# The keys' sums of a linear-attention kernel: rounded parts, two tiles behind the projections

## The reference, cut to what matters

```
k  = einsum('bnd,dhk->bnhk', x, Wk)                 # "key", 1024 columns a token
dd = einsum('bnhd,md->bnhm', k * dn, proj)          # "dash", 1024 columns a token
kf = exp(dd - sum(k*k)*dn*dn/2 - max(dd)) + eps     # features, 1024 a token
kv = einsum('bnhm,bnhd->bhmd', kf, v)               # v = x @ Wv
ks = sum(kf, axis=1)
```

## Time and profile before

| | us |
|---|---|
| median of 3 runs | 1642.57 (1641.53 to 1649.5) |
| profiled execution, its own time | 1645.18 |
| profiled execution, span of the trace | 1643.5 |
| TensorE busy | 1479.6 (90%) |
| VectorE busy | 1167.2 (71%) |
| ScalarE busy | 698.2 (42%) |
| GpSimd busy | 536.0 (33%) |
| keys' block, first DMA to last VectorE instruction | 513.37 to 869.32 |

### The profile page before, as it was taken

How to read it: one execution, slowest core, us unless ns; L and a number is a source line. 1 busy time by engine, 2 the same in 40 slices (tenths; PEclk the granted TensorE clock), 3 DMA queues, 4 the chain that set the end, 5 groups by cost and what they waited for, 6 DMA issues and landing times. The chain is left out here.

```text
span 1643.5 us, 23406 instructions
## 1 busy us (share of the span) xinstructions
PE 1479.6 (90%) x8607; PEld 1219.5 (74%) x8607; DVE 1167.2 (71%) x2252; ACT 698.2 (42%) x1291; POOL 536.0 (33%) x520
## 2 busy tenths in 40 slices
PE   8876659999991899999986999999998999989997
PEld 6443549999991666666645788888887889979996
DVE  6665885774003678878638878787886888899995
ACT  2054125546552132222222333333345777767774
POOL 2412025555551022222314000000004555547666
PEclk8877669999995799999998999999999999999999
DMA  6544819999954011111013000000103100000001
GB/s 205 232 162 163 282 59 277 269 294 277 286 137 138 26 39 39 39 39 39 26 52 115 1 26 27 26 26 27 65 13 93 52 27 14 1 1 27 14 27 39
DMA packets 121777, 152.00 MB, mean 92 GB/s; under 512 B 13584, under 2 KB 89528, under 8 KB 120640
## 3 DMA queue, kind: packets, MB, share of 16 engines
q1 hardware_dynamic: 108448, 129.55, 24.0%
q0 software_dynamic: 9216, 12.59, 4.3%
q10 hardware_dynamic: 4000, 8.37, 1.4%
HBM read 116.10 MB, written 33.60 MB: 91 GB/s over the span
## 5 line engine op out<-in xcount | busy, mean ns | idle before, releaser
L2357 POOL TENSOR_TENSOR ff_hid_lo<-ff_hid,ff_hid_hi 128x512 fp32r<-128x512 f32 x128 | 174.3, 1365 | 159.1 <-ACT ff_hid_hi L2269 157.7
L1230 PE MATMUL h_ps<-xT,w 128*128 128x128 f32 x1536 | 203.9, 287 | 1.1 <-ACT xT L938 1.1
L1230 PEld LDWEIGHTS h_ps<-xT,w 128*128 128x128 f32 x1536 | 191.0, 199 | 9.5 <-issue 9.5
L2638 PE MATMUL ff_down<-ff_w_hi,ff_hid_hi 128*128 128x256 f32 x512 | 146.8, 287 | 7.6 <-POOL ff_hid_lo L2357 4.5
L2639 PE MATMUL ff_down<-ff_w_lo,ff_hid_hi 128*128 128x256 f32 x512 | 145.3, 284 | 0.0
L2640 PE MATMUL ff_down<-ff_w_hi,ff_hid_lo 128*128 128x256 f32 x512 | 145.2, 284 | 0.0
L1344 PE MATMUL k_ring<-w_hi,hT_hi 128*128 128x512 f32 x256 | 120.0, 469 | 10.7 <-DVE hT_lo L1504 6.4
L1685 PE MATMUL k_acc<-wide_rows,hk 128*128 128x512 f32 x256 | 119.7, 599 | 4.5 <-ACT wide_rows L1629 4.5
L1111 DVE TENSOR_TENSOR yT<-yT_ps,b2T 128x256 f32<-128x256 f32 x48 | 20.4, 425 | 140.4 <-PE yT_ps L1244 137.3
L1344 PE MATMUL q_ring<-w_hi,hT_hi 128*128 128x512 f32 x256 | 109.9, 429 | 9.9 <-PEq L99 6.8
L2044 PE MATMUL q_out_ps<-kv_sums,wide_rows 128*128 128x256 f32 x512 | 115.5, 379 | 0.0
(11 more groups left out here) (436 smaller groups left out, 3620.4 us busy)
## 6 DMA issues: line engine op xcount, KB each, us to landing
w<-in_L_ffn_W_dram SPq DMA_DIRECT2D x48, 1024.0 KB, 6.0
w<-in_L_ffn_W_dram SPq DMA_DIRECT2D x48, 256.0 KB, 7.8
expert_sum_dram<-f_zero SPq DMA_DIRECT2D x8, 1024.0 KB, 15.3
x<-in_L_attn_x_dram SPq DMA_DIRECT2D x4, 1024.0 KB, 13.2
h_dram<-hg SPq DMA_DIRECT2D x8, 512.0 KB, 2.9
hk<-expert_sum_dram SPq DMA_DIRECT2D x8, 512.0 KB, 4.5
hT_hi<-expert_sum_dram SPq DMA_DIRECT2D x8, 512.0 KB, 5.4
h_dram<-hk SPq DMA_DIRECT2D x8, 512.0 KB, 6.1
```

The source lines that it names most:

```text
L1230: last = pe.matmul(h_ps[:, e % 2, s * KD + c, :], w1[:, e % RING, s, k, c::KD], xT[:, e % 2, k, :], start=(k == 0), stop=(k == KD - 1))
L2357: pool.tensor_tensor(hid_lo[:, m % PARTS, :], hid[:, m % WHOLES, :], hid_hi[:, m % PARTS, :].bitcast(F32), ALU.subtract).then_inc(part_low, 1)
L2638: pe.matmul(into, hid_hi[:, m % PARTS, tile], high[:, c, :], start=(c == 0 and j % 2 == 0), stop=False)
```

## The change

In the keys' block:

- `sums` takes f32 operands no more. ACT rounds the features into `features_hi` (`feature_high`) and the rows into `hk_hi` (`rows_high`); GpSimd subtracts to get `features_lo` (`feature_low`), DVE to get `hk_lo` (`rows_low`), both in place of the features and rows. A sum is then `split_products`, three products of parts for one f32 product.
- The sums of a tile stand two tiles later: `late = n * G + j - 2`. A counter `tile_summed` per tile replaces `sums_done` per group. `features_hi` has room for two tiles.
- The maximum over partitions is made by TensorE (`peak_turn`, `spread_peak`) in place of GpSimd. `turn(n+2)` stands before the last dash of the window, `total(n-1)` in window n.
- Group 0 is made ready tile by tile (`tile_sums` and so on), group 1's rows are joined on GpSimd (`group_sums`).

Outside it: the keys' weights are loaded and cut during the last experts (`key_high`, `key_low`), the experts' block ends without a drain of GpSimd, constants of the networks are made during the experts (`wave_angles`, `elu_rows`), the ring of expert weights is shifted by three slots, and in the queries' block GpSimd's products and sums wait for `normed` and come in smaller pieces.

The core of the diff:

```
-                    if n >= KV_RING:
-                        sp.wait_ge(sums_done, n - KV_RING + 1)
+                        sp.wait_ge(tile_summed, (n - KV_RING + 1) * G)
                         sp.wait_ge(h_out[n % KV_RING], 16 * (n // KV_RING))
                     sp.dma_start(hk[:, n % KV_RING], rows(g.expert_sums[0])).then_inc(first_in[n % KV_RING], 16)
...
                 for n in range(NG):
-                    peak_of(n)
                     if n + 2 < NG:
                         power(n + 2)
-                    add_features(n)
+                    add_first(n)
+                    if n < NG - 1:
+                        feature_low(n, 0)
+                        feature_low(n, 1)
+                    for j in range(2, G):
+                        add_feature(n, j)
+                        if n < NG - 1:
+                            feature_low(n, j)
...
+                def feature_low(n, j):
+                    pool.wait_ge(e_high_done, n * G + j + 1)
+                    pool.tensor_tensor(e_low[:, n % 2, j, :], dash[:, n % 2, j, :], e_high(n * G + j).bitcast(F32),
+                                       ALU.subtract).then_inc(e_low_done, 1)
...
+                def feature_high(n, j):
+                    i = n * G + j
+                    act.wait_ge(exp_done, i + 1)
+                    if i >= 2:
+                        act.wait_ge(tile_summed, i - 1)
+                    act.activation(e_high(i), dash[:, n % 2, j, :], ACT.Copy).then_inc(e_high_done, 1)
...
-                def sums(n, j, k):
+                def sums(i, k):
+                    n, j = i // G, i % G
                     if k == 0:
-                        pe.wait_ge(exp_done, n * G + j + 1)
+                        pe.wait_ge(e_low_done, i + 1)
...
-                        last = pe.matmul(acc[:, k, cols], hk[:, n % KV_RING, j, k * P:(k + 1) * P], dash[:, n % 2, j, cols],
-                                         start=(j == 0), stop=(j == G - 1))
+                        last = split_products(pe, acc[:, k, cols], rows, features, cols, j == 0, j == G - 1)
+                    if k == KD - 1:
+                        last.then_inc(tile_summed, 1)
...
                 for n in range(-1, NG):
                     for j in range(G):
-                        i = (n + 1) * G + j
+                        i, late = (n + 1) * G + j, n * G + j - 2
                         if n + 1 < NG:
                             project("key", i, key_done)
-                        if n >= 0 and j:
-                            sums(n, j - 1, 0)
+                        if n >= 0 and j == 0:
+                            peak_turn(n)
+                        if j == G - 1 and n + 2 < NG:
+                            turn(n + 2)
+                        if late >= 0:
+                            sums(late, 0)
+                        if n >= 0 and j == 0:
+                            spread_peak(n)
+                            if n:
+                                total(n - 1)
                         if n + 1 < NG:
                             project("dash", i, dash_done)
-                        if n >= 0 and j:
-                            sums(n, j - 1, 1)
+                        if late >= 0:
+                            sums(late, 1)
```

More of the change, by code:

```diff
@@ L596, with wave_tables @@
 FOLD_SLOT, ELU_SLOT, WAVE_SLOT = 3, 5, 7
+CONSTS_AT = 32
+B1, THETA, W_RE, W_IM, AMP, SINE, COSINE = range(7)
+TURN = 1.0 / (2.0 * 3.141592653589793)
+FULL = 6.283184
+STEP = 0.1 * TURN
+def wave_tables(g):
+    part = g.flip[:, 0:2 * CF].rearrange("p (i c) -> p i c", i=2)
+    return [part] + [g.flip[:, 2 * CF + i * CF * B:2 * CF + (i + 1) * CF * B].rearrange("p (c b) -> p c b", b=B) for i in range(3)]
 def expert_choice(nc, mk, g, a):
@@ L1359, in key_ring_order @@
 def key_ring_order():
-    order = [("turn", 0)]
+    order = []
     for n in range(-1, NG):
@@ new lines, in _ @@
+                tile_sums(0)
+                tile_statistics(0)
+                tile_sums(1)
+                tile_rows(0)
+                tile_statistics(1)
+                tile_sums(2)
+                tile_turned_low(0)
+                tile_rows(1)
+                tile_statistics(2)
+                tile_sums(3)
+                tile_rows(2)
+                tile_turned_low(1)
+                tile_statistics(3)
+                diag(0)
+                shift(0)
+                tile_rows(3)
@@ L1587, in _ @@
+                tile_turned_low(2)
+                for n in range(-1, NG - 1):
                     for j in range(G):
                         i = (n + 1) * G + j
-                        diag(i)
-                        shift(i)
-                        if n >= 0 and n + 2 < NG:
-                            if j == 0:
+                        if i:
+                            diag(i)
+                        if j == 0 and n >= 0:
+                            refer(n)
+                            if n:
+                                add_total(n - 1)
+                        if j == G - 1 and n + 2 < NG:
+                            turned_low(n + 2)
+                        if i:
+                            shift(i)
+                        if i == 1:
+                            tile_turned_low(3)
+                            v.mark(dve.tensor_reduce(f.h_sum[:, 0, :], first_sum[:].rearrange("p j k -> p k j"), AX.X, ALU.add))
+                        if j == 0 and n >= 0:
+                            rows_low(n)
+                        if j == 1 and n >= 1:
+                            add_sums(n - 1)
+                        if n + 2 < NG:
+                            if n < 0 and j == 1:
+                                dve.wait_ge(summed, 3)
+                                statistics(1)
+                            elif n < 0 and j == 2:
+                                rows(1)
+                            elif n < 0:
+                                pass
+                            elif j == 0:
@@ L1602, in _ @@
+                refer(NG - 1)
+                add_total(NG - 2)
+                rows_low(NG - 1)
+                add_sums(NG - 2)
+                for j in range(G):
+                    last_feature_low(j)
+                for i in range(2, 4):
+                    weights_low(i, next_raw)
+                turned_low(NG)
                 add_sums(NG - 1)
+                add_total(NG - 1)
             @block.scalar
@@ L1642, in _ @@
                             turned_high(n + 2)
-                turned_high(NG)
+                        if n >= 0:
+                            feature_high(n, j)
+                        if j == G - 1 and n + 1 < NG:
+                            rows_high(n + 1)
                 act.wait_ge(next_in, 32)
@@ L1654, in take, with tile_turn @@
                         kind, i = order[u - 2]
-                        pe.wait_ge(freed[kind], i + 1)
+                        pe.wait_ge(freed[kind], i if kind == "turn" else i + 1)
+                def tile_turn(j):
+                    pe.wait_ge(tile_h, j + 1)
+                    for k in range(KD):
+                        last = pe.transpose(first_turn[:, j, k], hk[:, 0, j, k * P:(k + 1) * P], g.ident[:])
+                    last.then_inc(tile_turned, 1)
                 def turn(n):
```

423 lines of the change are left out of this document (267 added, 156 removed).

## The result

The changed kernel takes 1782.45 us (median of 4 runs, 1780.64 to 1784.17), the kernel before 1642.13 (4 runs, 1641.53 to 1649.5). The ratio is 1.0834, with a 95% interval of 1.0812 to 1.0857: slower by 140 us, where 161 were forecast. The profiled execution of the changed kernel has a span of 1782.4 us.

What follows compares the result with a forecast made beforehand. TensorE was taken as the bound, 38.4 us a window; new waits make windows 1 to 5 +158 us, and all terms +161 on 1645.2 give 1806, less 2.6 for the median: 1803 us, range 1735 to 1838.

Steps and rivals of the forecast that it cites:

- start, to the end of window -1: Keys' block opening: missing drain gives 4 us, then 48 us from the loads; 558 against 565.9, so -8 us.
- window 0: First full window: no wait for the load but one for power's, slow restarts; 54 us against 37.4, +16.6.
- windows 1 to 5: Keys' block: five windows of 70 us each against 38.4, +158 us.
- queries and networks: Later stages: GpSimd's pieces no longer meet VectorE's, constants made earlier, less ScalarE's cuts of weights; -3 us.
- cycle: Windows 1 to 5, one D1 to the next: waits in a row, 70.5 us counted, 70 taken, bounds 59.5 and 75.5.
- D1: End of the dash of tile 1 in a window, from which the forecast times each step; D2, D3 likewise for tiles 2, 3.
- restart at the lower clock: TensorE after each idle time: 6.1 us at half speed, 3 us of work lost.
- rows beside GpSimd: VectorE's rows(n+2), 3.9 us with GpSimd idle, plus two waits of 2.5 for GpSimd's instructions; bounds none and four.
- saving of the products: TensorE's sums: 16 f32 products a window replaced by products of parts, 2.8 us off, 36.1 us a window if nothing waits.
- waits as forecast, but clock and port cost nothing: Rival, 12%: no lower clock or port waits; windows of 59.5 us, window 0 of 43, total 1740.
- the load isn't waited for: Rival, 10%: only power ahead of the low parts holds TensorE; cycle 59.4 us, total about 1750.
- Faster: Rival, 8%: low parts and loads in time, low part 0 within 4.1 us of D1; windows 36.1 us, total 1616.

Runs made afterwards that it cites:

- e0: The kernel before, unaltered, run and profiled a second time: 1642.53 us, span 1640.8.
- e1: Changed kernel with VectorE's both_sums(n+2) moved behind the shift of tile 1 and add_sums, directly ahead of join(n+2): 1751.83 us.
- e4: Changed kernel with the experts' first part landing in the free half of hT_lo, both loads issued at the window's start: 1732.15 us.
- e13: Changed kernel with 36 useless TensorE products ahead of tile 0's first half sum in each window from 0 on, except window 6: 1769.72 us.
- e6: Changed kernel with loads issued at the window's start, VectorE's calls reordered and GpSimd's power between the low parts of tiles 0 and 1: 1639.35 us.
- e10: e6 with rows_low a window earlier behind tile 2's shift, rows_high one tile sooner, tile 0's first half sum behind tile 2's dash: 1634.44 us.
- e11: e10 with GpSimd's power(n+2) back at the head of its list for the window: 1653.99 us.
- e9: Changed kernel with the queries' GpSimd additions again four of 128 x 2048 that start at once, without waits for normed: 1789.21 us.

## Why the prediction was right, and where it was off

By its own steps, with the profiled executions (in us; the change from the first profile of the kernel before, and from the second, e0's):

| step | forecast | against the first | against e0's |
|---|---|---|---|
| start, to the end of window -1 | -8 | -2.8 | -8.8 |
| window 0 | +16.6 | +12.0 | +14.9 |
| windows 1 to 5 | +158 | +149.3 | +149.3 |
| window 6 | -3 | -2.6 | -2.6 |
| the block's end | 0 | -1.0 | -2.0 |
| queries and networks | -3 | -16.0 | -9.2 |
| sum | +161 | +138.9 | +141.6 |

**The cycle was right step by step.** From D1, forecast and measured in the window shown: landing taken up 7.5 and 7.0; statistics done 19.3 and 19.0; low part 0 done 25.5 and 24.7; D2 32.5 and 31.0; rows done 43.9 and 41.5; D3 51.9 and 48.8; next D1 70.5 and 68.1. TensorE's two idle times are 20.6 (some 21) and 6.3 (7.3). That both waits in the chain are real, and that they come one behind the other, e1 to e4 show: taking either away gives 6.8 to 10.3 us a window, both together 17.2 and, with the rows in time, 27. The queue of VectorE cost what its rows said, and `feature_low`, 2.6 taken between 2.4 and 6.7, is 2.33.

**Two terms of the cycle were too large.** The restart at the lower clock was priced at 3 us, half of the 6.1 us at clock 0.50 in the earlier trace rows. Those rows are right, with 14 products at half speed behind waits of 4.29 and 2.77 us, but they don't carry over. Here it costs 2.1: ten products 0.43 apart where 0.23 would do, and a period 2.1 us shorter in e13. In e6 and e10 it costs 1.6. What sets the number was not tried; it doesn't grow with the wait in front. The first restart of the window shown:

```profile
724.80:729.40 4.60, 4.58 (x11) 3.63 (x12) 0.00 (x0) 0.00 (x0) 4.60 (x2) 0.52 0.00 0
729.40:735.40 6.00, 5.96 (x26) 4.53 (x25) 4.12 (x4) 1.06 (x2) 1.56 (x2) 1.00 0.00 0
```

And the rows beside GpSimd were priced at two waits of 2.5: the four TENSOR_SCALAR took 5.52 for 1.38, so 4.1 were lost. The four began at 733.55 and the last ended at 739.07, 0.5 us behind the second of the two GpSimd instructions that stand there back to back (733.88 and 736.21): VectorE was held by both. The Trainium skill (SBUF — State Buffer, Who interferes with whom) adds that reductions never contend; the trace agrees, with 1.23 us for the one of e11 at 709.09, beside GpSimd's addition of 708.45 to 710.85. The prediction's bound of 15 us for the rows, had each of the six instructions met one of GpSimd, wasn't reached: 8.0.

**The saving of the products was too large by a quarter.** Window 6 of the changed kernel, full and at full clock, is 35.76 us without a turn, where the one before, with a turn of 0.87 in it, was 38.4. So a window's work on TensorE is 36.6 us, not 36.1: 1.75 less than before, where 2.3 were counted. This changes little in the forecast's cycle, whose length the waits set, but it lowers what the change could ever give: some 12 us, not 16, in seven windows.

**The start was right by its own steps.** From the last scatter's issue to the keys' first load it was 10.6 us (502.79 to 513.37, and 10.5 in e0) and is now 6.1, so the missing drain gave what was counted. From the loads to the end of window -1 it is 47.1 where 52.5 were, and 48 forecast. Against the first profile this shows as only 2.8 us, because the experts' first gather is 7.6 us later in the changed kernel's. e0 shows that this is an execution's own, since the kernel before has it at 224.09 too, and against e0 the start gives 8.8.

**Queries and networks were undercounted.** 16 us against 3 in the first pair of profiles; against e0 it is 9.2 (queries 362.2 to 358.6, networks 404.2 to 398.7). Some 4 to 7 are the GpSimd pieces (e9). Part of the rest is the networks' opening, where TensorE waited 6.1 us for ScalarE's turned rows in the first profile and 3.3 in e0's, and now 1.0. The constants stood on VectorE in that opening and are now made among the experts; the prediction priced their instructions and not who queues behind them. That they are the cause was not tried.

So the sign, the place and the mechanism were right. Of the 22 us between forecast and measured sum, by the first profile, 9 are the cycle of windows 1 to 5 with its two prices, 5 window 0 with the same prices and a start some 1.5 us shorter, 13 the later stages and 1 the block's end; the start takes 5 of them back. The rival "waits as forecast, but clock and port cost nothing" (1740) is refused by e13 and by the 5.52; "the load isn't waited for" (1750) by e1 and e4. "Faster" (1616) named the right place, the low part within 4.1 us of D1, but no kernel here reached it: e6, with its three changes of order and an earlier landing, and e10 have that wait gone and stay at 1639 and 1634.

## What to carry to other kernels

When work is made to lag behind its producer, list what its completion used to release (here a buffer, and with it a load) and time that from the new place; then list what stands behind the late item on each in-order engine, because the wait is paid by all of them in a row. An operation that waits for a long chain belongs behind the ready work on its engine, not ahead of it. And when one engine is nearly full, taking a wait away uncovers the next: a short wait of TensorE can be paid twice, once as idle time and once in clock (2.4 and 1.6 us a window in e10).

## What the runs showed of the hardware

- A short wait can be enough for the lower clock: behind waits of 2.06 us (e6, from the fifth product on) and 2.44 us (e10) TensorE's products started 0.43 us apart, though it had been busy without a pause for over 30 us ahead. What the lower clock then costs doesn't grow with the wait: 14 products at half speed behind waits of 2.77 and 4.29 us (kernel before), ten behind 20.61 (changed kernel), eight or nine behind 2.06 and 2.44. In the changed kernel's opening a wait of 1.81 us was not followed by it:

```profile
542.51 0.50 PE L1422 MATMUL k_ring<-w_hi,hT_hi 128*128 128x512 f32 x1 [1.81 <-DVE hT_lo L1637]
542.85 0.39 PE L1423 MATMUL k_ring<-w_lo,hT_hi 128*128 128x512 f32 x1
543.08 0.39 PE L1424 MATMUL k_ring<-w_hi,hT_lo 128*128 128x512 f32 x1
```

- Where GpSimd's work falls matters more than how much there is: the same instructions in another order (e11 against e10) cost VectorE 5.9 us a window at the rows instead of 1.1 there and 2.1 at `both_sums`, and 19.6 us in all.
- The kernel before has stages that differ by 2 to 7 us between its two profiled executions, while their spans differ by 2.7 (1643.5 and 1640.8): an outer term of 5 us can't be read from one pair of profiles.
